# Graph layer on one core: the small products of two gather groups stand together behind the fp32 products of both

## What is computed

```python
H = gelu(X @ W1.T + b1)
X_src = H[src]
W_tar = gelu(X_src @ WA.T) @ WB.T                  # 4 mix factors
cross = X_src[:, :, None] * W_tar[:, None, :]      # edges x 128 x 4
agg = gelu(segment_sum(cross, dst))                # per destination node
out_edge = einsum('ehm,em->eh', agg[dst], W_tar)
agg_node = segment_sum(out_edge, dst) / max(count(dst), 1)
out = gelu(concat([agg_node, H])) @ W2.T + b2      # and x is added
```

## Time and profile before

| | |
|---|---|
| three runs | 1298.65, 1301.7, 1304.33 us |
| profiled execution | 1304.83 us, its span 1303.1 us, mean granted clock 0.927 |
| PE busy | 1070.4 us (82%) |
| POOL busy | 903.8 us (69%) |
| DVE busy | 947.6 us (73%) |
| chain that ended last | PE 46%, DVE 17%, POOL 14%, issue 10%, DMA 7%, ACT 5% |

### The profile page before, as it was taken

The page is one execution under the profiler, slowest core; times in us unless marked ns, Lnnn a source line. Parts: engine busy times, 40 slices in busy tenths (PEclk is TensorE's granted clock), DMA queues, the critical chain, the costliest instruction groups (busy, mean ns, idle before and its releaser), DMA issues.

```text
span 1303.1 us, 25372 instructions
## 1 busy us (share of the span) xinstructions
PE 1070.4 (82%) x7395; PEld 727.5 (56%) x7395; DVE 947.6 (73%) x2601; ACT 604.1 (46%) x1304; POOL 903.8 (69%) x923
## 2 busy tenths in 40 slices
PE   5665127789999989999999999899999997889558
PEld 3454013356767656666666666566666654566324
DVE  7998558888888668888678887578887763532147
ACT  6765664436666445656445655356655200000224
POOL 4766657667777777777777777777777777767037
PEclk9867559989999999999999999999999998999859
DMA  5244552226666655555655555655555567655422
GB/s 206 100 161 190 227 208 56 54 76 169 181 167 175 179 156 164 156 156 156 187 164 157 157 163 159 179 151 156 155 156 152 158 197 163 201 139 161 119 76 83
DMA packets 83891, 201.11 MB, mean 154 GB/s; under 512 B 21917, under 2 KB 33375, under 8 KB 81553
## 3 DMA queue, kind: packets, MB, share of 16 engines
q1 hardware_dynamic: 58282, 142.37, 34.9%
q0 software_dynamic: 25472, 57.11, 18.1%
HBM read 167.18 MB, written 32.22 MB: 153 GB/s over the span
## 4 chain that ended last, share of the span: by engine, by line
PE 46%; DVE 17%; POOL 14%; issue 10%; DMA 7%; ACT 5%; DVEq 2%; SPq 0%; ACTq 0%; POOLq 0%
PE ps L1398 19%; POOL q L664 12%; PE ps L1379 11%; PE ps L1351 10%; DMA q<-node_table,src_g 4%; PE ps L1354 3%; DVE big L1084 2%; PE ps L1403 2%; DVE q L1093 1%; ACT hot_b L800 1%; DVE big L1280 1%; DVE mask L1059 1%; DVE big L1015 1%; DVE big L1029 1%; DVE q L948 1%
## 5 line engine op out<-in xcount | busy, mean ns | idle before, releaser
L664 POOL DMA_INDIRECT q<-node_table,src_g x796 | 770.1, 968 | 273.2 <-issue 216.6
L1398 PE MATMUL ps<-big,q 128*128 128x298 bf16 (+2 forms) x2940 | 464.0, 297 | 0.0
L800 ACT ACTIVATE hot_b<-iota_b,q 128x128 bf16<-128x128 bf16 x847 | 269.7, 389 | 343.8 <-PE ps L1379 343.6
L1351 PE MATMUL ps<-mask,q 128*128 128x96 f32 x1592 | 254.4, 283 | 76.7 <-DVE mask L1059 75.4
L1398 PEld LDWEIGHTS ps<-big,q 128*128 128x128 bf16 x2940 | 264.7, 98 | 82.7 <-issue 2.7
L1093 DVE TENSOR_SCALAR q<-iota_a,q 128x490 bf16<-128x490 f16 (+1 forms) x847 | 269.3, 365 | 24.7 <-issue 12.5
L1379 PE MATMUL ps<-q,hot_b 128*128 128x490 bf16 (+1 forms) x847 | 233.9, 372 | 58.5 <-ACT hot_b L803 25.0
L1351 PEld LDWEIGHTS ps<-mask,q 128*128 128x128 f32 x1592 | 216.7, 194 | 112.2 <-DVE mask L1059 100.7
L1084 DVE TENSOR_TENSOR big<-big,ps 128x490 f32 (+1 forms) x358 | 232.4, 649 | 55.1 <-PE ps L1379 53.8
L1059 DVE TENSOR_TENSOR mask<-eq,q 128x192 f32<-128x192 bf16 x398 | 141.5, 356 | 124.2 <-DMA q<-node_table,src_g 97.0
L1379 PEld LDWEIGHTS ps<-q,hot_b 128*128 128x128 bf16 x847 | 69.9, 97 | 161.4 <-DVE big L1084 61.4
(11 more groups left out here) (134 smaller groups left out, 776.9 us busy)
## 6 DMA issues: line engine op xcount, KB each, us to landing
q<-product_parts SPq DMA_DIRECT2D x245, 388.0 KB
product_parts<-big SPq DMA_DIRECT2D x12, 1552.0 KB, 5.9
q<-node_table,src_g POOLq DMA_INDIRECT x796
node_table<-big SPq DMA_DIRECT2D x12, 280.0 KB, 3.1
own_part<-big SPq DMA_DIRECT2D x12, 256.0 KB, 2.9
big<-own_part SPq DMA_DIRECT2D x3, 1024.0 KB, 10.0
out_dram<-q SPq DMA_DIRECT2D x12, 256.0 KB, 2.0
dense_columns<-q SPq DMA_DIRECT2D x3, 596.0 KB
```

The source lines that it names most:

```text
L664: pool.indirect_dma_start(out=ring[:, t % R, :], out_offset=None, in_=table, in_offset=bass.IndirectOffsetOnAxis(ap=src_g[:, t:t + 1], axi ...
L800: last = nc.scalar.activation(hot_b[:, b % 2, i, :], iota_b[:, :], ACT.Abs, bias=nkey_b[:, t:t + 1])
L1351: nc.tensor.matmul(o[:, 0:MIX * W], ring[:, s + t, 0:D], mask[:, b, t, :, :], start=(t == 0), stop=(t == G - 1))
L1398: last = nc.tensor.matmul(ps[:, 3 + m, 0:n], c[:, LEAD + P * (MIX * part + m):LEAD + P * (MIX * part + m + 1)], counts[k % 2][:, a, c0:c1] ...
```

## The change

`sum_group` is split in two functions. The fp32 products of each group stay where they were. The small products of an even group are no longer issued behind its own fp32 products, but behind those of the next, odd group: four small products in a row, the even group's two first. If the odd group stands in a later slot, the even group's small products, and with them its `group_summed`, move behind the count products and the unit between. The fallback path at the end (`general_path`) is unchanged in its order.

```diff
-            def sum_group(o, b, e, s):
+            def sum_products(o, b, s):
                 for t in range(G):
                     nc.tensor.matmul(o[:, 0:MIX * W], ring[:, s + t, 0:D], mask[:, b, t, :, :],
                                      start=(t == 0), stop=(t == G - 1))
+
+            def sum_factors(o, e, s):
                 for t in range(G):
                     last = nc.tensor.matmul(o[0:NP, MIX * W:SLOT], ring_b[:, s + t, TP:TP + NP],
                                             eq[:, e, t, :], start=(t == 0), stop=(t == G - 1))
...
-                    sum_group(group_psum(g, 0, SLOT), g % MB, g % EB, G * g % R)
+                    sum_products(group_psum(g, 0, SLOT), g % MB, G * g % R)
+                    for f in range(g - 1 if g % 2 else g, g + 1) if g % 2 or g == NG - 1 else ():
+                        sum_factors(group_psum(f, 0, SLOT), f % EB, G * f % R)
```

More of the change, by code:

```diff
@@ L1410, in step @@
                         pe.wait_ge(masks_ready, GPS * n + NG + j + 1)
-                        sum_group(ps[:, GBANKS[j % MS], 0:SLOT], j % MS, j % MS, G * j)
+                        sum_products(ps[:, GBANKS[j % MS], 0:SLOT], j % MS, G * j)
+                        sum_factors(ps[:, GBANKS[j % MS], 0:SLOT], j % MS, G * j)
                 general_path(pe, step)
```

## The result

The changed kernel takes 1309.35 us (median of 20 runs, 1304.54 to 1313.18) against 1302.39 us for the kernel before (median of 20, 1298.65 to 1310.42). The ratio is 1.0046, 95% interval 1.0034 to 1.0059: some 6 us slower. The forecast was 1303.5 us, +1.8 us, in a range of 1293 to 1313. The sign is right and the time lies in the range, but the forecast step is only about a third of the measured one. The experiments show that two terms of its sum were far too small, a loss and a gain, and cancelled in part: that the forecast came so near is partly luck.

What follows compares the result with a forecast made beforehand. The prediction took POOL's pace of about 1.25 us per gather as the bound in stages 1 to 3 and most of 5. It summed 2.3 + 2.5 - 3 = +1.8 us on the median 1301.7, giving 1303.5 us, range 1293 to 1313.

Steps and rivals of the forecast that it cites:

- The bound: Stages 1 to 3 and most of 5: POOL's pace of about 1.25 us per gather bounds, not PE's work.
- The prediction's own sign of being wrong: Wrong altogether if a stage from 1 to 3 gets more than 3 us shorter.
- PE's saving: On PE: 0.24 us for each of 70 pairs in one slot, 0.08 for each of 129 in two; 27 us less work.
- Where the saving reaches the end: Only in stage 4, where PE saves 5.3 us: 3 us gained, bounds 0 and 5.3; nothing in stages 0 to 3.
- The cost of the late release: POOL's gather for odd group g+5 waits until g+1 is multiplied; costs only where the ring catches POOL: 2.3 + 2.5 us.
- kinds 1 and 2: Ring losses with both groups in one slot, or in two slots with PE running: one loss, 2.5 us, bounds 0 and 12.5.
- Behind the check: After `check_bounds` in stage 5: the gather for group 376 is 2.3 us late, and nothing takes it back.
- The wide gain: Rival: PE's time counts more widely, winning half of POOL's 17.5 us of real waits: 1295 us; chance 0.14.
- The unsaved boundary: Rival: the fp32-to-bf16 boundary on PE is not saved, no stage-4 gain: +4.8 us, 1306.5 us; chance 0.13.
- The short ring: Rival: POOL's waits before odd groups' gathers decide, four losses beside the check's: +10.8 us, 1312.5 us; chance 0.25.
- Its sign: POOL's waits for small products growing by more than 10 us beyond the check would show the shorter ring decides.

Runs made afterwards that it cites:

- Experiment 3: Small products left out entirely, the last fp32 product raising `group_summed`, against the kernel before: 1300.06 us, ratio 0.9972.
- the late release alone: PE's order as in the kernel before, only `group_summed` of a pair raised at the odd group, by two: 1321.41 us against 1304.04, ratio 1.0145.
- the late check: `check_bounds` moved from slot 24 to 44 of stage 5, behind the last gather; usual speed, against the kernel before: 0.9943 without the change, 0.9966 with it.

## Why the prediction was right in sign and short in size

- **The bound.** Right as far as it was tested. Experiment 3 shows that PE's work is not the bound: some 100 us less of it, 4 us won. That POOL's pace of 1.25 us is the bound in its place rests on the rows. The prediction's own sign of being wrong did not appear: in the changed kernel no stage from 1 to 3 became shorter from its first unit to the next stage's (168.5, 194.6 and 193.3 us, before 165.3, 193.7 and 192.9).
- **PE's saving.** A pair in one slot 0.24 us, right. A pair in two slots was taken at 0.08 "by the nearer row", the epilogue's boundary; the count product follows the fp32 pass after one step, so the first group saves 0.22, and the whole is 0.22 less two more small products, 0.025 us each in the trace's starts (the four together last 0.26 where two lasted 0.20): 0.17. The sum is 70 x 0.24 + 129 x 0.17 = 39 us, not 27. The loads of the small products begin with the products and not before, here too (weight loads, same place as above):

```profile
607.59 0.15 PEld L1356 LDWEIGHTS ps<-eq,q 128*13 128x13 bf16 x4
```

  So the rule of the Trainium skill (TensorE: Matmul & The Clock Gate, Step-by-step: what each phase is for) that PE pulls weight loads ahead does not describe these narrow loads behind fp32 passes. What the error of 12 us in PE's work did to the end by itself was not measured.
- **Where the saving reaches the end.** Mis-sized. The sum had -3 us, in stage 4; that stage is 1.3 us shorter in the profile (197.9 us from its first unit to that of stage 5, before 199.2). Over the whole kernel the saving weighs more. Between the late release with and without it, it is worth 13 us. I had asked what PE's time is worth in the kernel before (experiment 3: about 4 us for a much larger saving) and not in the kernel as it would be, where an even group's release hangs on PE's progress through another slot.
- **The cost of the late release.** Mis-sized in the other direction, and this is the step that failed: "Of kinds 1 and 2 ... I count one loss of a group, 2.5 us". With the check's 2.3 that made 4.8 us, and the runs show 17 for the release alone. The error was to count the places where POOL idles. POOL's pace is just enough, so a lead that is lost stays lost even where POOL never idles long: with the late release alone the gathers are 3.5, 5.6 and 8.0 us behind at 361, 668 and 749. POOL's waits hardly show it (55.6 us before, 51.4 changed, 59.3 with the late release alone). The masks' waits for gathers rose, but experiment 3 shows that they are no price for it.
- **Behind the check.** Right in mechanism and too small: 2.3 forecast, 2.7 in the trace from the check's end, but 5.7 over the whole stop, and 3 to 6 by the table of experiment 3. That nothing takes it back is right: from the gather for 376 to the last one POOL needs 54.0 us, before 53.9. What was not forecast is that the check also began 4.4 us later against the stage's start (1134.95 - 1038.15 = 96.8 us, before 92.4), 3.1 of them against POOL's gathers. The check stands behind the mask of group 369, and that one waited 4.13 us for its gather (1.25 before). How much of it is lost lead and how much a gather that landed late in this execution, the runs don't settle.
- **The rivals.** The wide gain is refuted by experiment 3. The unsaved boundary is refuted by the rows of the new order; the saving of 0.17 lies just above the 0.07 to 0.16 that the prediction gave. The short ring, at a chance of 0.25 and +10.8 us, is the mechanism that the runs at the usual speed point to; with PE's saving against it, it ends at +6. Its sign, 10 us more of POOL's waits beyond the check, did not show; it was a poor sign, since POOL's waits hardly hold such a loss. The measured time lies between forecast and this rival.

## What to carry to other kernels

An instruction that both finishes a result and frees a buffer has two prices. Before moving it behind other work to save switches, count what the buffer's filler loses. A filler that runs at its full pace hardly shows it in its own waits, and its consumers' waits for data grow as well when they only ask sooner. Compare when the same fill starts in both traces. When a saving and a delay hang on the same engine, price each without the other (a kernel that moves only the release, one that only drops the work): the small sum hid a loss of 17 us and a gain of 13. And a long run of one engine in the middle of a pipeline with little slack is worth moving to where the pipeline has ended.

## What was not expected

- The step from an fp32 pass to a bf16 product with 128 stationary columns cost nothing (0.11 us, the pitch of the fp32 passes), to the products with 13 stationary columns 0.20 us, and the next product after two of those started 0.13 us behind the first. In the epilogue, 0.35 us lay between the last fp32 pass (128 columns) and the bf16 product. The row that was nearest by type did not tell the cost at this place.
- On one chip all kernels ran 17% slower (before 1529.88 us), with PE idle for up to 4 us where the profile shows no wait. What caused it is not shown. With the late check in both kernels the same change cost 2.4% there and 0.2% at the usual speed.
